# A gated graph network: tile 1's first transposed state from TensorE, ScalarE and VectorE instead of the transposing DMA

## What is computed

```python
h = jnp.maximum(_layernorm(x, axis=-1), 0.0)
A = (adj != 0).astype(x.dtype)
for l in range(5):
    m = jnp.einsum('bnd,de->bne', h, weight[l])
    agg = jnp.einsum('bij,bid->bjd', A, m)
    gi = agg @ w_ih.T + b_ih;  gh = h @ w_hh.T + b_hh
    r = sigmoid(i_r + h_r);  z = sigmoid(i_z + h_z)
    n = tanh(i_n + r * h_n)
    h = (1.0 - z) * n + z * h
return x + h * nodemask[..., None]
```

## Time and profile before

| | us |
|---|---|
| median of the runs | 371.98 |
| profiled execution, time | 371.11 |
| profiled execution, span | 369.2 |
| TensorE busy | 360.0 |
| VectorE busy | 322.8 |
| ScalarE busy | 299.8 |
| POOL busy | 263.6 |

### The profile page before, as it was taken

How to read it: one execution, slowest core, us unless ns; L and a number is a source line. 1 busy time by engine, 2 the same in 40 slices (tenths; PEclk the granted TensorE clock), 3 DMA queues, 4 the chain that set the end, 5 groups by cost and what they waited for, 6 DMA issues and landing times.

```text
span 369.2 us, 6528 instructions
## 1 busy us (share of the span) xinstructions
PE 360.0 (98%) x2125; PEld 181.1 (49%) x2125; DVE 322.8 (87%) x588; ACT 299.8 (81%) x495; POOL 263.6 (71%) x261
## 2 busy tenths in 40 slices
PE   7999999999999999999999999999999999999992
PEld 3455555544454555555545455555545555555541
DVE  4977898899889999999999999999998988787886
ACT  5997788998879988888877889899877767777753
POOL 3765758889578878787656878888756777755574
PEclk9999999999999999999999999999999999999998
DMA  8634443857662693939624384756834543349522
GB/s 245 211 59 86 115 97 76 170 126 151 152 115 45 147 180 78 228 68 200 169 42 105 64 197 85 164 123 158 151 94 112 130 99 59 89 100 231 124 57 85
DMA packets 108512, 46.03 MB, mean 125 GB/s; under 512 B 97728, under 2 KB 98112, under 8 KB 108480
## 3 DMA queue, kind: packets, MB, share of 16 engines
q1 hardware_dynamic: 108336, 45.37, 55.3%
q10 hardware_dynamic: 144, 0.26, 0.2%
HBM read 17.57 MB, written 4.19 MB: 59 GB/s over the span
## 4 chain that ended last, share of the span: by engine, by line
PE 90%; DVE 4%; DMA 2%; POOL 2%; issue 1%; ACT 1%; DVEq 0%; POOLq 0%
PE ps_r L293 9%; PE ps_z L294 9%; PE ps_z L293 9%; PE ps_r L294 9%; PE ps_z L295 9%; PE ps_r L295 9%; PE ps_s L366 5%; PE ps_s L367 5%; PE ps_in L295 4%; PE ps_hn L294 4%; PE ps_in L293 4%; PE ps_in L294 4%; PE ps_hn L295 4%; PE ps_hn L293 4%; DMA hp<-nat 1%
## 5 line engine op out<-in xcount | busy, mean ns | idle before, releaser
L816 POOL TENSOR_TENSOR zh<-z,h 128x512 f32<-128x512 f32 x80 | 101.9, 1273 | 81.4 <-ACT z L484 81.3
L478 ACT ACTIVATE r<-ps_r,b_sum,unscale 128x512 f32<-128x512 f32 x80 | 62.2, 778 | 37.9 <-PE ps_r L295 37.5
L488 ACT ACTIVATE ps_in<-ps_in,b_ih,unscale 128x512 f32<-128x512 f32 x80 | 60.1, 751 | 22.3 <-DVE ps_in L630 21.3
L821 POOL TENSOR_TENSOR hp<-h,hp 128x512 f16<-128x512 f32 x64 | 74.1, 1157 | 0.0
L624 DVE SCALAR_TENSOR_TENSOR rhn<-ps_hn,b_hn,r 128x512 f32<-128x512 f32 x80 | 59.8, 748 | 10.3 <-ACT r L478 9.8
L630 DVE TENSOR_TENSOR ps_in<-ps_in,rhn 128x512 f32<-128x512 f32 x80 | 56.0, 700 | 11.5 <-PE ps_in L295 6.7
L484 ACT ACTIVATE z<-ps_z,b_sum,unscale 128x512 f32<-128x512 f32 x80 | 61.6, 770 | 0.7 <-PE ps_z L295 0.7
L641 DVE TENSOR_TENSOR h<-zh,ps_in 128x512 f32<-128x512 f32 x76 | 52.2, 687 | 8.5 <-DVE ps_in L636 0.5
L636 DVE SCALAR_TENSOR_TENSOR ps_in<-z,ps_in 128x512 f32<-128x512 f32 x79 | 54.7, 692 | 5.6 <-ACT ps_in L488 5.6
L618 DVE TENSOR_TENSOR s_lo<-ps_s,s_hi 128x512 f16<-128x512 f32 x80 | 54.4, 680 | 0.4 <-ACT s_hi L472 0.4
L472 ACT CAST s_hi<-ps_s 128x512 f16<-128x512 f32 x80 | 46.6, 583 | 0.0
(11 more groups left out here) (115 smaller groups left out, 745.0 us busy)
## 6 DMA issues: line engine op xcount, KB each, us to landing
x_in<-in_x SPq DMA_DIRECT2D x16, 256.0 KB, 3.8
adj_in<-in_adj SPq DMA_DIRECT2D x16, 256.0 KB, 3.4
x_out<-in_xT SPq DMA_DIRECT2D x16, 256.0 KB, 3.1
mask_in<-in_mask_row SPq DMA_DIRECT2D x16, 256.0 KB, 3.8
out<-x_out SPq DMA_DIRECT2D x15, 256.0 KB, 2.7
nat<-hp SPq DMA_TRANSPOSE x64, 3.1
fold_in<-in_fold_lhs SPq DMA_DIRECT2D x1, 320.0 KB, 3.9
out<-x_out ACTq DMA_DIRECT2D x1, 256.0 KB, 2.1
```

Source lines behind the costliest of these rows:

```text
L478: nc.scalar.activation(r[:], ps_r[:], ACT.Sigmoid, bias=b_sum[:, 0:1], scale=unscale[:, 0:1]).then_inc(r_done, 1)
L488: nc.scalar.activation(ps_in[K % 2][:], ps_in[K % 2][:], ACT.Tanh, bias=b_ih[:, 2:3], scale=unscale[:, 0:1]).then_inc(n_done, 1)
L816: nc.gpsimd.tensor_tensor(zh[:, K % 2], z[:, K % 2], h[:, t % RING], ALU.mult).then_inc(zh_done, 1)
L821: nc.gpsimd.tensor_tensor(h_lo(t), h[:, t % RING], h_hi(t), ALU.subtract).then_inc(h_lo_done, 1)
```

## The change

Tile 1 goes the direct way like tile 0. Its DMA transpose and TensorE's wait on it go. ScalarE gets `transposed_high(1)` between the sigmoid r of unit 0 and `natural_high(2)`; VectorE gets `transposed_low(1)` ahead of `r_times_hn(0)`. `transposed(1)` keeps its place and now also waits for `transposed_low(1)`, and unit 1's products wait on `h_lo_init`. The semaphore count for ring slots follows `DIRECT` by itself.

```diff
-DIRECT = 1
+DIRECT = 2
...
                 if K < N - 1:
                     gate_r(K)
                     if K == 0:
+                        transposed_high(1)
                         natural_high(2)
...
                 if K == 0:
                     layernorm(3, 0)
                     layernorm(3, 1)
+                    transposed(1)
                 else:
                     gate_n(K)
                 if folding(K):
                     v_high(folding(K))
-                if K < FIRST - 1:
+                if 0 < K < FIRST - 1:
                     transposed(K + 1)
...
             first()
             for K in range(N):
+                if K == 0:
+                    transposed_low(1)
                 r_times_hn(K)
```

## The result

Six runs of the changed kernel gave a median of 373.62 us (372.95 to 373.96), six of the kernel before 372.13 us (371.76 to 372.46): ratio 1.0039, 95% interval 1.0026 to 1.0052. The change costs 1.5 us. The sign was forecast, the size was not: 0.86 us, and 373.62 lies above the range's upper end of 373.4.

What follows compares the result with a forecast made beforehand. TensorE, 98% busy and practically without slack from 27.35 us, bounds the kernel. Delays at its meeting points don't add up; only unit 3's last and largest, 0.86 us, stays: 371.98 + 0.86 = 372.84, say 372.8 us (+0.23%), range 372.0 to 373.4.

Steps and rivals of the forecast that it cites:

- `shift`: POOL's step for tile 3, waiting for the negated mean: starts at 17.92 us, holding ScalarE's layer norm 0.86 us late.
- The critical chain: Copy, low half, `rhn`, negated mean, POOL's `shift`, layer norm, `nat` and DMA of tile 3: unit 3 0.86 us late.
- B: Rival: only ScalarE's own step is lost, +0.6 us or less, 372.2 to 372.6; chance 0.17.
- C: Rival: not slower, the removed DMA wait counts; -0.46 us at most, 371.5, else 372.0; chance 0.10.
- E: Rival: added waits let TensorE's clock fall, +2.1 us on top, about 375; chance 0.03.
- D: Rival: VectorE's full 1.17 us reaches unit 3 or hand-overs cost more; +1.15 to +1.4, 373.1 to 373.4; chance 0.10.
- 22.40 + 5.51 = 27.91: When TensorE would reach unit 3 without waiting for tile 3's DMA, against 28.21 us with that wait.
- tile 2's DMA: Hidden before by some 0.4 us, it now ends a TensorE wait; unit 2 starts 0.5 to 0.6 us late.
- the one on unit 3: SP issues tile 3's DMA at 25.11 us, so TensorE starts unit 3 at 28.21 instead of 27.35, 0.86 late.
- from there the same 76 units in the same time: TensorE's stream behind unit 3 keeps its length, covers unchanged, and carries the 0.86 us to the end.
- The bounds: Copy's earliest start -0.15, four hand-overs -0.12 to +0.12, copy's length +0.05: together +0.59 to +1.03 us.
- 0.72 us for the copy: Skill-page estimate for ScalarE's 512-element copy; the measured row's 0.58 us was used instead; by the page 1.00 us in sum.

Runs made afterwards that it cites:

- mean_first: Changed kernel with tile 3's negated mean moved ahead of tile 1's low half on VectorE; median 373.42 us, ratio 1.0053 to the kernel before.
- dve_only: Kernel before plus an unread extra half on VectorE where the change puts its low half, met waits on ScalarE (16) and VectorE (4); 372.68 us, ratio 1.0030.
- pad_dve_after: Changed kernel plus 4 already met waits (2 instructions) at the start of VectorE's queue; 373.05 us, ratio 1.0044 to the kernel before.
- pad_both_after: Changed kernel plus already met waits on ScalarE (16, 8 instructions) and VectorE (4, 2 instructions); 372.54 us, ratio 1.0029 to the kernel before.
- act_only: Kernel before plus an unread extra copy of tile 1's transposed state on ScalarE, with 16 met waits on ScalarE; 372.64 us, ratio 1.0032.
- pad8_before: Kernel before plus only 16 already met waits (8 instructions) on ScalarE, meant as a control; 372.08 us, ratio 1.0018 to the kernel before.

## Why the prediction was wrong

**What held.** With 0.49 us taken off, the steps of the changed profile against those forecast: copy 15.79 (15.81), low half 16.49 (16.44), `rhn` 17.10 (17.04), negated mean 17.76 (17.71), `shift` 18.00 (17.92), layer norm 18.23 (18.17), unit 1 17.24 (17.17), `nat` of tile 3 at 23.17 (23.19), issue of tile 3's DMA 25.09 (25.11), 0.84 us late. The critical chain was the right one, and the rivals B, C and E don't fit: mean_first and dve_only show that `shift` bites, unit 1's wait grew, and the spacing of the matmuls stayed at 0.22 us at a granted clock of 1.00. D had nearly the right size (+1.15 to +1.4 against 1.43 at unit 3) for reasons that didn't occur: VectorE's full delay reached unit 3 in no profile, and the steps behind the hand-overs came within 0.08 us of the forecast. The sign was right for the reason given, the later issue.

**Two slips without effect.** "22.40 + 5.51 = 27.91" counts the 0.09 us of wait that stands ahead of unit 3 in the kernel before; without it the sum is 27.82. And the forecast had TensorE wait for tile 2's DMA and start unit 2 at 22.35 to 22.44 us. It started at 22.54 (23.03 - 0.49) without a wait, since the halt had made TensorE later than the DMA; in pad_dve_after, without the halt, the wait is there with 0.17 us. Unit 3's wait absorbed both.

**The first step that failed** is the one on unit 3: "SP issues at 25.11, TensorE starts at 28.21 instead of 27.35". It took the DMA's 3.10 us as a constant. It took 3.69, since a packet of ScalarE's code fell into its later part. The fourteen profiles decide it: with the packet inside, 3.46 to 3.75 us in eight of them, with it outside, 3.07 to 3.10 in six, whichever version of the program it is. The change put the packet there by two more instructions in ScalarE's queue: +0.6 us.

**The second** is "from there the same 76 units in the same time", with all covers counted as unchanged. One more instruction in VectorE's queue moved its halts onto instructions that wait for their predecessor, in units 0, 26 and 51. The one in unit 0 made unit 1's second half start at 19.70 instead of the forecast 19.13 us (19.30 in pad_dve_after, where it is gone) and was absorbed by unit 3's later wait; the other two cost TensorE 0.23 and 0.25 us in a stream without slack: +0.5 us. Padding took both effects away (pad_both_after: unit 3 0.83 us late, no late gaps), and what is left is the forecast's 0.86.

**The bounds** asked what the added instructions cost as work, and not what it costs that they exist. A range that allowed for one such half microsecond would have reached 373.9.

The Trainium skill's budget from which the prediction estimated 0.72 us for the copy (ScalarE: Activation LUTs, section Rules for kernel authors) is stated there for an ACTIVATE whose bias is a pointer operand. The copy has no such bias, so the estimate was too high for it; it took 0.60 us. The Trainium skill's 390 ns for a 128x128 transpose on TensorE against 1309 ns by DMA (VectorE: DVE Perf Modes, section The three transpose paths) have no gain to show here, as tile 1's transposes stood on TensorE before.

## What to carry to other kernels

Where one engine's stream has no slack, a wait taken off it is worth only as much as the latest of the waits behind it allows: here the removed 0.37 us would have been absorbed by tile 3's DMA in any case, while what was added stood in front of the very chain that feeds that DMA. Look in the queues of the other engines for small instructions behind the place where something is inserted (a negated mean of 0.16 us carried VectorE's delay over to ScalarE). And when a change of well under 1% comes out half a microsecond off, compare the code packets and the numbers of the instructions that halt before you look for a cause in the work: padding with waits that are already met separates the two. Look in each profile whether it did what it was put in for: in act_only, dve_only and pad8_before ScalarE's padding left the packet in the DMA.

## What the runs showed of the hardware

- VectorE halted for 0.43 to 0.51 us at instructions 64, 192, 320, 448, 576 and 704 of its queue, counted from 1 in the profile with wait-only ones; it was seen only where such an instruction depends on the one before it.
- A packet of program code that came 1.7 to 2.4 us behind the issue of tile 3's transposing DMA went with 3.46 to 3.75 us from issue to TensorE (8 profiles), without it 3.07 to 3.10 us (6 profiles). One that came 0.5 to 0.6 us behind tile 2's issue cost nothing (2 profiles).
- The same program, measured twice in one group, differed by a ratio of 1.0031 (1.0014 to 1.0047). In the profiles, when the first weights landed moved the first product by up to 1.34 us.
- Added work on two engines in one place delayed tile 3's issue by 0.56 us by the one part, 0.77 by the other and 0.84 by both.
- VectorE's adjacency comparison of tile 3 took 0.46 us before. In the seven profiles in which it started while POOL's z*h ran, it ended 0.28 to 0.29 us behind z*h each time, and took up to 1.43 us.
